# GpSimd clears an unread tile once for every six gathers, in a two-layer GNN kernel on one core

## The reference

```python
# block 1: graph layer, over the edges
t1 = feat @ W1;  msg = t1[src] + feat[src] * feat[dst] @ W2
agg = segment_sum(msg / (sqrt(out_deg[src]) * sqrt(out_deg[dst])), dst)
x = x + normalize(leaky_relu(t1 + agg + b))        # feat = ln(x)
# block 2
x = x + ln(x) @ weight.T + bias
# block 3: graph layer with relations, over the edges
m = linear(h[src] * rel[edge_type], msg_w, msg_b) * gate(rel[edge_type]) * norm(src, dst)
x = x + linear(h + segment_sum(m, dst), upd_w, upd_b)   # h = ln(x)
# block 4: feed-forward on the top rows of a router score
x = x + where(selected, gelu(ln(x) @ w1 + b1) @ w2 * score, 0)
```

## Time and profile before

| | |
|---|---|
| median of 3 runs | 5586.52 us |
| lowest and highest | 5573.98 and 5605.82 us |
| the profiled execution | 5576.72 us |
| its span, from first to last instruction | 5574.6 us |
| mean granted clock of TensorE | 0.837 of full speed |

### The profile page before, as it was taken

The page is one execution under the profiler, slowest core; times in us unless marked ns, Lnnn a source line. Parts: engine busy times, 40 slices in busy tenths (PEclk is TensorE's granted clock), DMA queues, the critical chain, the costliest instruction groups (busy, mean ns, idle before and its releaser), DMA issues.

```text
span 5574.6 us, 70515 instructions
## 1 busy us (share of the span) xinstructions
PE 3870.7 (69%) x21018; PEld 3013.8 (54%) x21018; DVE 2860.3 (51%) x11695; ACT 1615.1 (29%) x6417; POOL 3281.5 (59%) x3447
## 2 busy tenths in 40 slices
PE   6556555555555555555568888888888888888886
PEld 6544444444444444444445666666666666666664
DVE  8745555555555555554544444444444444444444
ACT  3145444544454545454500111111111111111111
POOL 0166666666666666666556665655666666666661
PEclk9577777777777778777779999999999999999998
DMA  4333333333333333333344444444444444444442
GB/s 97 117 96 99 97 98 95 99 93 96 97 97 94 99 98 98 97 97 92 84 115 113 110 111 108 109 105 110 106 112 110 107 112 108 109 110 113 110 109 74
DMA packets 275018, 571.62 MB, mean 103 GB/s; under 512 B 86331, under 2 KB 164376, under 8 KB 274642
## 3 DMA queue, kind: packets, MB, share of 16 engines
q0 software_dynamic: 164640, 456.82, 32.3%
q1 hardware_dynamic: 98162, 101.78, 5.9%
q10 hardware_dynamic: 11840, 8.50, 0.5%
HBM read 539.92 MB, written 26.92 MB: 102 GB/s over the span
## 4 chain that ended last, share of the span: by engine, by line
PE 43%; DVE 25%; another core or an unknown queue 22%; issue 8%; ACT 2%; DMA 1%; DVEq 0%; SPq 0%; PEldq 0%; ACTq 0%
PE psE L700 17%; PE psY L681 7%; PE psT L681 6%; DVE both L1328 6%; DVE work L1402 4%; DVE work L1398 3%; PE psE L894 3%; PE psE L875 2%; ACT work L1066 2%; DVE work L1250 2%; PE psY L657 1%; PE psE L763 1%; DVE work L1345 1%; DVE st L1459 1%
## 5 line engine op out<-in xcount | busy, mean ns | idle before, releaser
L594 POOL DMA_INDIRECT work<-t_d,srci x3430 | 3273.6, 954 | 2192.6 <-issue 1265.5
L700 PE MATMUL psE<-work,both 128*128 128x257 f32 x6860 | 2125.6, 431 | 840.1 <-issue 405.2
L700 PEld LDWEIGHTS psE<-work,both 128*128 128x128 f32 x6860 | 1338.9, 217 | 1131.7 <-issue 477.5
L1066 ACT ACTIVATE work<-work 128x35 f16<-128x35 bf16 x5145 | 1131.0, 311 | 701.7 <-DVE work L1398 554.1
L1398 DVE TENSOR_SCALAR work<-iob,work 128x35 bf16<-128x35 bf16 x1715 | 268.9, 251 | 965.0 <-remote 776.2
L1328 DVE TENSOR_SCALAR both<-iof,dstf 128x128 f32<-128x128 f32 x3430 | 727.9, 296 | 27.6 <-remote 14.4
L1345 DVE TENSOR_TENSOR work<-work,psT 128x257 f32<-128x257 f32 x858 | 342.4, 420 | 714.3 <-PE psT L681 263.9
L1345 DVE TENSOR_TENSOR work<-work,psY 128x257 f32<-128x257 f32 x857 | 341.7, 419 | 668.4 <-PE psY L681 223.3
L681 PE MATMUL psT<-relb,work 125*128 125x257 bf16 x3381 | 541.9, 283 | 24.1 <-issue 24.0
L681 PE MATMUL psY<-relb,work 125*128 125x257 bf16 x3381 | 546.5, 285 | 2.5 <-issue 2.4
L681 PEld LDWEIGHTS psT<-relb,work 125*128 125x128 bf16 x3381 | 340.5, 101 | 195.7 <-issue 43.3
(11 more groups left out here) (260 smaller groups left out, 3274.5 us busy)
## 6 DMA issues: line engine op xcount, KB each, us to landing
work<-t_d,srci POOLq DMA_INDIRECT x3430
work<-types_d SPq DMA_DIRECT2D x245, 218.8 KB
both<-acc_d SPq DMA_DIRECT2D x98, 130.0 KB
t_d<-accf SPq DMA_DIRECT2D x7, 910.0 KB, 9.2
acc_d<-work ACTq DMA_DIRECT2D x1, 6370.0 KB
t_d<-accf SPq DMA_DIRECT2D x49, 130.0 KB
X<-in_x SPq DMA_DIRECT2D x1, 6144.0 KB
out<-X SPq DMA_DIRECT2D x6, 896.0 KB
```

The lines of the kernel that those rows point to most:

```text
L594: pool.indirect_dma_start(gath[:, n % RG, :], None, table, bass.IndirectOffsetOnAxis(ap=srci[:, n:n + 1], axis=0)).then_inc(s_g[n % RG], 16)
L700: ins = nc.tensor.matmul(psE[:, b % 2, 0:DW], sel[:, third, k % SG, :], gath[:, n % RG, 0:DW], start=False, stop=(k == C - 1))
L1066: ins = nc.scalar.activation(to_s3[:, n % 2, i, j, :], to_s[:, n % 2, i, :], ACT.Copy, scale=load3[:, b // RB % 2, j, w:w + 1])
```

## The change

A new tile `idle` of 128 x 640 bfloat16 takes the place of `zb`. In both passes, ahead of the gathers 6, 12, ... 1710, GpSimd clears it and raises a new semaphore `s_pause`. Ahead of a clear it waits until the previous clear, six gathers back, has ended (the first clear waits for nothing). The clear stands ahead of the gather's own wait for `s_mm`. There are 285 clears in a pass, 570 in all. The one clear of `zb` at the start is gone, and the three engines that wait for the constants wait for 10 in place of 11.

```diff
+BURST = 6
...
-        zb = sb("zb", [P, P], BF16)
+        idle = sb("idle", [P, 640], BF16)
...
+        s_pause = sem("s_pause")
...
-            pool.memset(zb[:, :], 0.0).then_inc(s_const, 1)
...
             def gathers(layer, table):
                 for n in range(SLOTS):
+                    if n > 0 and n % BURST == 0:
+                        pause = layer * (SLOTS // BURST) + n // BURST
+                        if pause > 1:
+                            pool.wait_ge(s_pause, pause - 1)
+                        pool.memset(idle[:, :], 0.0).then_inc(s_pause, 1)
                     if n >= RG:
                         pool.wait_ge(s_mm, summed(layer * SLOTS + n - RG + 1))
...
-            pe.wait_ge(s_const, 11)
+            pe.wait_ge(s_const, 10)
```

More of the change, by code:

```diff
@@ L1017, in _ @@
                 act.dma_start(t[:, :], a.rearrange("(o a) c -> o (a c)", o=1).broadcast_to([P, D])).then_inc(s_w, 16)
-            act.wait_ge(s_const, 11)
+            act.wait_ge(s_const, 10)
             act.wait_ge(s_x, 32)
@@ L1213, in _ @@
             v.memset(zero, 0.0).then_inc(s_zero, 1)
-            dve.wait_ge(s_const, 11)
+            dve.wait_ge(s_const, 10)
             link(v.tensor_scalar(starts[:, 0:NB], iof[:, 0:NB], float(P), None, ALU.mult))
```

## The result

The changed kernel takes 5508.19 us in the median of 4 runs (5505.19 to 5511.06), the kernel before 5590.20 us beside it. The ratio is 0.9854, with a 95% interval of 0.9824 to 0.9883. A later group of runs gave 0.9852 (0.9814 to 0.9889). The prediction said 5595 us and no change, with a range of 5562 to 5640 us: it was wrong, on the side to which it had given 0.12.

What follows compares the result with a forecast made beforehand. TensorE and its handshake with VectorE were taken to bound both passes. Set-up -0.15, clears on GpSimd 1 and VectorE's slowing 8 made 9 us on the 5586.5 us median: 5595 us, no change, range 5562 to 5640.

Steps and rivals of the forecast that it cites:

- The price of a clear: GpSimd's queue, both passes: a clear costs 0.57 to 1.25 us, taken as 0.87, in all 248 us a pass.
- The order on GpSimd: Rival, clears and gathers wait for each other: 2.3 us a clear, 408 us more, 5990 us; chance 0.08.
- What hides it: GpSimd's stalls for TensorE and gathers seven slots early cover the clears; 0 to 3 us remain, taken as 1.
- The threshold: GpSimd becomes the bound when a clear costs over 1.34 us in the first pass, 1.83 us in the second.
- The ports: VectorE's one-hot lines, slowed by a clear's SBUF writes: 0 to 45 us, taken as 8.
- the first rival: Clears block VectorE at lines 1328, 1398 and 1402 of the first pass: 45 us slower, 5632 us; chance 0.15.
- The passes are bounded by TensorE and its handshake with VectorE: Both passes: gathers are early, GpSimd is second to the bound at 85% and 80% of what it can issue.
- A third of it that it can't name: First pass's chain of waits: VectorE's three lines 24.6%, TensorE, and a third that the chain can't name.
- The faster rival: Pauses help: later gathers miss VectorE's bursts, or TensorE's clock is granted more; 30 us faster, 5556 us; chance 0.12.
- later gathers fall out of VectorE's busy bursts: First of two mechanisms by which the pauses would make the kernel faster, 30 us together; chance 0.12.
- a sign that I was wrong: Either pass: a granted clock, 0.75 and 0.92 before, that moves by over 0.02.

Runs made afterwards that it cites:

- the narrow clears: The changed kernel with clears of 2 columns in place of 640; 1.0008 in the 4705 us group, 1.0015 in the 5591 us group, against the kernel before.
- the 32-partition clear: The changed kernel with the 640-column clear on 32 of the 128 partitions, a quarter of the bytes; 0.9860 against the kernel before.
- the two pauses without a long clear: Changed kernel, clears replaced by a wait for the last gather but one to land (1.0011), or by sixteen 2-column clears each (0.9992), against the kernel before.
- the sixteen short clears: The changed kernel with sixteen clears of 2 columns in place of each one of 640; 0.9992 against the kernel before.
- the half kernel: The kernel before, with line 700 multiplying 128 of the 257 columns, gathers and waits the same; 5548 us, 0.9936 against the kernel before.
- the landing waits: Changed kernel without clears; once per six gathers GpSimd waits until the last gather but one has landed; 1.107 (4705 us group), 1.0011 (5591 us group) against kernel before.
- the landing kernel: The changed kernel without clears; once per six gathers GpSimd waits until the gather just issued has landed; 5865 us, 1.0349 against the kernel before.

## Why the prediction was wrong

**What held.** *The price of a clear.* Taken 0.87 us, with 0.57 us as the lower end: it is 0.65 us as an instruction and 0.51 us of GpSimd's queue, under the lower end, because the clear runs in part inside the 0.30 us that gathers leave idle anyway, while I had taken its whole duration as the least that it costs. *The order on GpSimd.* The clear and the gathers don't wait for each other: the clear at 1521.49 begins as the gather ends, and the next gather follows it by 0.16 us. *What hides it.* The waits of GpSimd took the clears up, and gathers stayed early. *The threshold.* GpSimd becomes the bound at a pause of 1.34 us in the first pass: a pause of 1.75 us and more made it so, one of 0.5 us did not. *The ports.* VectorE's lines 1328, 1398 and 1402 rose from 296, 251 and 285 to 321, 277 and 327 ns: the clear does meet them. The median of line 1328 stayed (281 and 280 ns), but its longest record grew from 524 to 1290 ns, with 960 columns to 1784, and with the narrow clears it was 525:

```profile
L1335 DVE TENSOR_SCALAR both<-iof,dstf x3430: 267/280/1290, 260.1 to 5399.3; 128x128 f32<-128x128 f32 x191
```

So some of these instructions are stopped for about a whole clear or more, and most never meet one. The trace agrees to that extent with the rule that the prediction took from "SBUF — State Buffer" of the Trainium skill, section "SBUF: two separate sides"; with the 32-partition clear, as long as the others, it agrees only in part (mean 305, longest 830 ns). But by my test ("up by 10 ns and more if the first rival is") the kernel should have been slower, and it was faster: the lines' cost on the chain was outweighed.

**The step that failed** is the one before the terms: "The passes are bounded by TensorE and its handshake with VectorE", taken as a pace that the clears can only leave or lengthen. The releases by TensorE were held fixed, so the sum had terms of 0 and above, and its lower bound was nothing. "A third of it that it can't name" stood in the same paragraph, and it is the only large part of the chain that fell: by 112 us in the first pass and by 170 in the second, where some of it is only named otherwise, against 123 us more in VectorE's lines. TensorE's completions come late by amounts that no record explains, and in the changed kernel VectorE waits less for them, by 108 and 96 us. The term that was missing is some minus 80 us; it was shown by the kernels with and without clears, not by the chain.

**The faster rival** had the right sign and 0.12. Its price of 30 us was too small, and neither of its mechanisms is shown. Against "later gathers fall out of VectorE's busy bursts" speak the two pauses without a long clear, 1.0011 and 0.9992, neither of them a clean test. The granted clock did rise, from 0.75 to 0.78 and from 0.92 to 0.93, in the first pass past the 0.02 that I had called a sign that I was wrong, but TensorE's busy time there rose from 1416 to 1449 us where that rival had it fall to 1361. And the 32-partition kernel has a mean of 0.843 with the gain, the sixteen short clears 0.851 without it, and the half kernel 0.775. So the clock doesn't carry the gain.

**What is shown and what is open.** Shown: the addresses, the semaphore, the place, the bytes written and a delay of VectorE do not give the gain; one clear of 0.65 us or more for six gathers does, in either pass, and with half of TensorE's columns too. Not quite shown: that the mere pause doesn't, for the landing waits starved the others at times, and the sixteen clears brought instructions of their own. Shown as well: the gain came only where gathers are early and TensorE's completions are late. Where the gathers were the bound, in the group of 4705 us, a clear cost its whole time on GpSimd. Not shown: by what path a long instruction on GpSimd makes TensorE's completions less late. The single matmuls 0.7 us apart point to TensorE getting its instructions slowly, which would fit that half the columns changed little. So would this wait of before, which stands in no profile of the group of 4705 us:

```profile
PE psE L700 <- issue: 405.2, 202, 13.7
```

But it is as long in the changed kernel (405.4 us), and no run here changed the number or the supply of TensorE's instructions, so this is an argument and not a finding.

## What to carry to other kernels

When a good part of the chain of waits has no name, the pace of the engine behind it isn't a constant, and a change elsewhere can move it either way: keep a term below zero in the sum and widen the range by the 1 or 2% that such a change was worth here. A gain that was found by trial, such as this, should be run on more than one chip and at more than one time: clears shifted by three gathers were worth 1.5% where TensorE was the bound and cost 6% where the gathers were. To part a pause from what makes it, hold the engine for the same time in two or three other ways, and look at what each of these adds of its own.

## What the runs showed of the hardware

The same program took 4705 us in one group and 5587 to 5671 us in the others, 19 to 21% more. In the four profiles of the group of 4705 us no wait was "remote"; in the profile of the kernel before VectorE's lines 1398 and 1345 waited 1206 us (776.2 + 429.8) for completions without a record, and in the landing kernel of the 5671 us group, where the gathers were the bound, all of VectorE's lines only 10 us. A clear on GpSimd beside VectorE's one-hots leaves their median at 280 ns and stretches the longest from 524 to 1290 ns (640 columns) and 1784 ns (960); on 32 partitions to 830 ns. A clear on GpSimd costs 0.51 us of its queue for 640 columns and 0.77 us for 960 behind a gather, about 0.8 ns a column, and 0.01 us for 2 columns (4.5 us over 570 of them, in the group where GpSimd was the bound).
